# Nine norms on one core: each token's variance in 8 partitions instead of 32

## The reference: what is computed

```python
def _layernorm(x, axis=-1, eps=1e-05):
    m = jnp.mean(x, axis=axis, keepdims=True)
    v = jnp.var(x, axis=axis, keepdims=True)
    return (x - m) / jnp.sqrt(v + eps)
...
def _rmsnorm(x, w):
    var = jnp.mean(x * x, axis=-1, keepdims=True)
    return x * jax.lax.rsqrt(var + EPS) * w
...
h = _layernorm(x, axis=-1) * (1 + ca) + sa
```

## Time and profile before

| | |
|---|---|
| time, median of 3 runs | 2621.33 us (2616.67 to 2623.15) |
| the profiled execution's own time | 2619.61 us |
| its span, first to last instruction | 2617.6 us |
| mean granted TensorE clock over the span | 0.898 of full speed |
| PE busy | 2235.2 us (85%) |
| DVE busy | 1773.8 us (68%) |
| ACT busy | 1517.4 us (58%) |

### The profile page before, as it was taken

One profiled execution on the slowest core, in us unless ns is written; L12 is line 12 of the kernel. 1 busy time (PEld: TensorE's weight loads), 2 busy tenths in 40 slices (PEclk: granted clock), 3 DMA queues, 4 the chain that ended last, 5 costly groups with the idle time before them and its releaser, 6 DMA issues. The chain is left out here.

```text
span 2617.6 us, 40655 instructions
## 1 busy us (share of the span) xinstructions
PE 2235.2 (85%) x14536; PEld 1008.3 (39%) x14544; DVE 1773.8 (68%) x3947; ACT 1517.4 (58%) x2345; POOL 361.0 (14%) x562
## 2 busy tenths in 40 slices
PE   4599999999994499999976996799999768979797
PEld 2344433444332143333333442333333334734473
DVE  5688888888834578787744555787778368437643
ACT  1068888888882028887742221188876533943592
POOL 3100000000000200011120002000011224303330
PEclk8589999999997659999987997599999888989897
DMA  4510200000000531010100003420101024613560
GB/s 155 100 30 7 33 8 11 13 7 13 4 4 2 133 49 27 11 29 15 29 17 1 0 0 109 62 36 12 28 12 27 21 80 155 216 35 129 169 186 17
DMA packets 78881, 130.26 MB, mean 50 GB/s; under 512 B 16496, under 2 KB 38768, under 8 KB 77168
## 3 DMA queue, kind: packets, MB, share of 16 engines
q1 hardware_dynamic: 75392, 117.62, 17.4%
q10 hardware_dynamic: 3312, 10.33, 1.4%
HBM read 53.13 MB, written 15.20 MB: 26 GB/s over the span
## 5 line engine op out<-in xcount | busy, mean ns | idle before, releaser
L794 ACT ACTIVATE att_probs<-psum 128x1024 f32<-128x1024 f32 (+3 forms) x1152 | 1035.1, 959 | 244.7 <-PE psum L846 242.8
L736 DVE TENSOR_REDUCE att_part_max<-psum 128x1 f32<-128x512 f32 x1312 | 840.8, 685 | 167.5 <-PE psum L828 165.4
L828 PE MATMUL psum<-k_rows,att_q_rows 64*128 64x512 f32 (+3 forms) x2304 | 739.5, 489 | 100.8 <-DMA att_q_rows<-q_pieces 60.5
L828 PEld LDWEIGHTS psum<-k_rows,att_q_rows 64*128 64x128 f32 x2304 | 350.9, 197 | 653.4 <-DVE att_part_max L736 279.3
L846 PE MATMUL psum<-att_q_rows,k_rows 64*128 64x512 f32 (+3 forms) x2304 | 453.0, 416 | 27.9 <-ACT att_probs L794 18.0
L871 PE MATMUL psum<-att_probs,v_aug 128*9 128x512 f32 (+3 forms) x3712 | 432.2, 539 | 0.5 <-POOL att_probs L674 0.3
L780 ACT ACTIVATE att_rise<-psum 128x512 f32<-128x512 f32 x240 | 144.4, 602 | 309.0 <-PE psum L828 275.4
L846 PEld LDWEIGHTS psum<-att_q_rows,k_rows 64*128 64x128 f32 x2304 | 237.2, 190 | 177.7 <-ACT att_probs L794 160.7
L733 DVE CUSTOM_DVE_ANT_0 att_masked<-psum,mask_max_sb 128x128 bf16<-128x128 f32 (+3 forms) x512 | 232.8, 485 | 54.7 <-PE psum L828 52.8
L725 DVE CUSTOM_DVE_ANT_0 att_rise<-psum,att_rise 128x512 f32<-128x512 f32 x240 | 166.1, 692 | 78.1 <-PE psum L828 49.1
L674 POOL TENSOR_SCALAR_AFFINE_SELECT att_probs<-att_probs 128x256 f32<-128x256 f32 x256 | 102.5, 406 | 800.3 <-ACT att_probs L794 797.7
(11 more groups left out here) (256 smaller groups left out, 2138.4 us busy)
## 6 DMA issues: line engine op xcount, KB each, us to landing
lproj_swapped<-lproj_other SPq DMA_DIRECT2D x128, 128.0 KB, 2.1
k_rows<-k_pieces SPq DMA_DIRECT2D x48, 320.0 KB, 10.9
latt_k<-local_k_T SPq DMA_DIRECT2D x32, 384.0 KB, 3.0
att_q_rows<-q_pieces SPq DMA_DIRECT2D x168, 64.0 KB
lproj_table<-in_tables SPq DMA_DIRECT2D x16, 512.0 KB, 4.2
latt_q<-local_q_T SPq DMA_DIRECT2D x32, 256.0 KB, 2.4
latt_v_seen<-local_v_tok SPq DMA_DIRECT2D x64, 128.0 KB, 2.4
latt_v_seen<-local_v_tok SPq DMA_DIRECT2D x32, 256.0 KB, 2.4
```

Of the source, the lines that this page charges most:

```text
L736: nc.vector.tensor_reduce(column, ring[e % NRING][:, 0:w], AX.X, ALU.max).then_inc(ring_free, 1)
L794: nc.scalar.activation(probs[s % NPROBS][:, pr, :, at:BANK], st[pr][:, :, at:BANK], ACT.Exp, scale=scale).then_inc(st_free, 1)
L828: nc.tensor.matmul(ring[e % NRING][:, 0:w], q_rows[u % NQ][rows, pr, qt * P:(qt + 1) * P].bitcast(F32R), k_rows[b][rows, pr, (kc + 1) * BA ...
```

## The change

The variance of a token is put in 8 partitions instead of 32. Chunk c's 32 partitions are shared by its four quarters of 128 tokens: quarter j goes to partitions 32c+8j to 32c+8j+7. The bank then holds 128 partitions by 128 columns, and so do `std` and `inv`.

To get there, the four variance matmuls over 512 columns become sixteen over 128 columns. Each has 32 weight columns, of which 8 are 1/128 and 24 are zero, and the four of a chunk accumulate in the same place. On the way back the four spread matmuls over 512 columns also become sixteen over 128 columns: those of quarter j pick row 8j of each chunk's 32, and each writes a quarter of the chunk's bank. Only the last quarter of a chunk releases DVE. `averages` grows from 128 by 384 numbers to 128 by 768.

```diff
-    centring, mean_rows, first_rows = averages[:, 0:P], averages[:, P:P + 32], averages[:, 2 * P:3 * P]
+    centring = averages[:, 0:P]
+    mean_rows = [averages[:, P + 32 * j:P + 32 * (j + 1)] for j in range(4)]
+    pick_rows = [averages[:, (2 + j) * P:(3 + j) * P] for j in range(4)]
...
-        std, inv, eps_col = sb("std", [P, BANK]), sb("inv", [P, BANK]), sb("eps", [P, 1])
+        std, inv, eps_col = sb("std", [P, P]), sb("inv", [P, P]), sb("eps", [P, 1])
...
-        var, spread = bank(psum, NC), [bank(psum, NC + c) for c in range(NC)]
+        var, spread = bank(psum, NC)[:, 0:P], [bank(psum, NC + c) for c in range(NC)]
...
-            for c in range(NC):
-                last = nc.tensor.matmul(var[32 * c:32 * c + 32, :], mean_rows, square[:, chunk(c)], start=True, stop=True)
+            for j in range(4):
+                for c in range(NC):
+                    at = c * BANK + j * P
+                    last = nc.tensor.matmul(var[32 * c:32 * c + 32, :], mean_rows[j], square[:, at:at + P], start=j == 0, stop=j == 3,
+                                            skip_group_check=True)
             last.then_inc(var_full, 1)
             pe.wait_ge(inv_done, 1)
-            for c in range(NC):
-                rows = slice(32 * c, 32 * c + 32)
-                nc.tensor.matmul(spread[c], first_rows[rows, :], inv[rows, :], start=True, stop=True).then_inc(spread_full, 1)
+            for j in range(4):
+                for c in range(NC):
+                    rows = slice(32 * c, 32 * c + 32)
+                    m = nc.tensor.matmul(spread[c][:, j * P:(j + 1) * P], pick_rows[j][rows, :], inv[rows, :], start=True, stop=True)
+                    if j == 3:
+                        m.then_inc(spread_full, 1)
...
-    c = {"ident": np.eye(P, dtype=f32), "averages": np.zeros((P, 3 * P), f32)}
+    c = {"ident": np.eye(P, dtype=f32), "averages": np.zeros((P, 6 * P), f32)}
     c["averages"][:, 0:P] = np.eye(P) - 1.0 / P
-    c["averages"][:, P:P + 32] = 1.0 / P
-    c["averages"][0::32, 2 * P:] = 1
+    for j in range(4):
+        c["averages"][:, P + 32 * j + 8 * j:P + 32 * j + 8 * (j + 1)] = 1.0 / P
+        c["averages"][8 * j::32, (2 + j) * P:(3 + j) * P] = 1
```

## The result

The changed kernel takes 2581.64 us (median of 4 runs, 2579.39 to 2586.22), the kernel before 2620.66 beside it (4 runs). The ratio is 0.9855, with a 95% interval from 0.9835 to 0.9874: 38 us less (33 to 43). Two later timings gave 0.9853 [0.9839, 0.9866] and 0.9870 [0.9848, 0.9891]. The forecast was 2593.4, with a range from 2586 to 2603. The direction was right. The gain is some 10 us larger than forecast, and the time is under the range.

A forecast was written before the change was run, and what follows sets the result against it. Each norm was taken as a serial chain with every microsecond on the path. Reciprocal 21.6, root 2.9, variance matmuls -0.4 and clock 3.8 sum to 27.9 us saved, giving a median of 2593.4 us, range 2586 to 2603.

The forecast's parts named there:

- The reciprocal: DVE's reciprocal in each norm: 128 columns instead of 512 take 0.95 us, not 3.35; nine norms save 21.6 us.
- The root: ACT's root in each norm: 384 columns fewer save 0.32 us, 2.9 in nine norms, at most 3.5.
- The variance matmuls: Sixteen matmuls in 8 rounds instead of 2 take 1.10 us, not 1.06; a cost of 0.4 us in all.
- The pacing rival: PE starts passes at a fixed pace, so variance matmuls take 1.58 us; about 2600 in total; chance 0.08.
- The spread: Spread matmuls, 8 rounds instead of 2: no change from 2.09 us at 1.2 GHz, weight loads hidden.
- The two rivals with visible or serial loads: Spread weight loads: visible in each strip, 3.82 us, about 2614, chance 0.04; or one after another, 7.3, about 2643, 0.02.
- The clock: Shorter PE idling before the spread keeps 2.4 GHz in some norms, saving 3.8 us, between 0 and 8.6.
- a shift that eats the gain elsewhere: Outside the norms, a shift cancels the gain; counted as no difference; chance 0.02.

The follow-up runs named there:

- 12: Changed kernel with unread filler matmuls between variance and spread, plus 140 more TensorE instructions in ln1b and 236 in lnf0; ratio 0.9965 to the kernel before.
- experiment 13: The changed kernel, unaltered, timed again as a base for later runs; 2585.25 us, ratio 0.9870 to the kernel before.

## Why the prediction was right and wrong

**The reciprocal** was to save 3.35 - 0.95 = 2.40 nine times, 21.6. It takes 952 to 954 ns in all nine: right to the figure, as the straight line through the earlier trace rows gave.

**The root** takes 368 ns, 0.32 less than the 687 of the earlier trace rows, 2.9 in nine: the value taken, with the bias as a fixed part.

**The variance matmuls** take 1.08 where 1.10 was forecast. The pacing rival (1.58) is out: 1.08 / 32 is 0.034 a pass. The Trainium skill's pace of some 62 ns a matmul with hardware decode off ("TensorE: Matmul & The Clock Gate", section "Wait — 56ns, not 53.3ns?") would make 32 of them 2.0 us, an estimate from that page. The trace does not show that pace; how the matmuls were decoded no run here shows.

**The spread** takes 2.09 at 1.2 GHz, as before, and 1.17 to 1.24 at 2.4 GHz, where 1.13 was counted. Its 32 loads of 128 weight columns are through in 0.98. The two rivals with visible or serial loads (3.82 and 7.3) are out. The Trainium skill ("TensorE: Matmul & The Clock Gate", Part 3, "The mechanism") says that a weight load overlaps matmuls in flight only where its row group differs. The trace disagrees: here eight loads follow each other in one row group, and the spread takes 0.04 to 0.11 us longer than the 1.13 of two rounds of 512 columns.

**The clock** was to give back 3.8: ln0b whole, six layer norms by half. It gave the whole in ln0a, ln0b and both lnf, part in ln1a, nothing in ln0z, ln1b and the RMS norms. The nine spreads took 9 x 2.09 = 18.8 and now take 14.9 by the groups above: 3.9. The sum is right, though not norm by norm, and the half was a guess between two rows, so that part is in some measure luck. It held in the two later profiles of the changed kernel (4.0 and 3.7), though ln0a took 1.17 and 1.91 there. With a loss of some 0.2 on the variance the four terms come to 28.2, against the 27.9 of the forecast. Over whole norms it is 26.3 in the profiled execution, because the centring ahead of two of them scatters: in lnf1 it took 6.60 us where it had taken 5.37.

**What failed** is the sum as a whole, in what it left out. The prediction took the norms for all that changes ("the norms are a small part of the span and nothing runs beside them"), gave the rest of the program no term, and let only scatter widen the range downwards. It had a case for "a shift that eats the gain elsewhere" (0.02), none for one that adds to it. But 24 more matmuls a norm are 864 more instructions, and a program has a place as well as a price: local layer 0 came to stand 672 later, 160 beyond a full fetch, and its attention went from 96.6 to 98.0 us down to 92.7 to 94.8. The three runs with the displacement but without the shorter steps put it at 6.6, 8.1 and 5.2 us (all three between 2.6 and 11). About 3.5 of that are seen in local layer 0 (189.2 to 189.5 against 184.8 to 186.5 in the runs at 160 and 167, leaving out 12 with its padding, but 188.4 in experiment 13); where the rest lies, or whether there is any, the scatter of the other stages hides. The forecast's 28 and these 5 to 8 are 33 to 36 us; the three measured gains are 34 to 39, with intervals of some 4 to 6 either way. So the step that failed is the term for the rest of the program, put at nothing: it was worth 5 to 8 us.

The Trainium skill speaks of this in "Runtime: NRT & Kernel Launch", section "Instruction fetch mechanics": each sequencer fetches its own next page of 16 KiB, 256 instructions, by DMA, and crossing into one is "mostly hidden". The trace agrees on the size (1.70 MB in 104 packets) and the step of 256. Hidden it is not where a load that PE waits for is in flight: by the means of the two groups, 97.4 against 93.0, that is some 4 us in one stage.

## What to carry to other kernels

A chain of dependent steps on one tile can be priced row by row, and such a sum held here, term by term, to 0.3 us of 28; narrowing a tile by moving its columns into partitions that held copies paid because root and reciprocal cost by the column (0.84 and 6.25 ns). But count instructions too: adding some moved every later fetch of that engine, and a stage that is tight on loads gained or lost 3 to 5 us by it, as much as a small optimisation is worth. Before a gain or a loss of some tenths of a per cent is put down to an edit, run the old kernel with as many idle instructions at that place, and compare stages, not only totals.

## What was not expected of the hardware

- Where some five fetches of TensorE's instructions (16 KB, 0.9 to 1.9 us each) fall moves a 93 us stage by 4 us in the mean (93.0 against 97.4), by 1 at the least (94.9 against 96.0). From some 33 to 77 us into the local attention, where the program loops, no fetch appears in any profile; the late loads are issued ahead of that stretch and behind it.
- A wait on a semaphore that has its value already cost PE's queue some 50 to 54 ns (255 in 12.8 us, 471 in 25.3). Idle instructions are free only while a gap covers them.
- Thirty-two float32 passes of 128 columns with a weight load each run in 1.08 us on four column strips (32 weight columns) and in 1.17 on four row strips (128 weight columns), 0.02 and 0.04 longer than two rounds of 512 (1.06, and 1.13 in the earlier trace rows).
